# Local attention: queries scaled on GpSimd together with the keys, a constant scale in the mask, loops at fixed places

## The reference

```
q, k, v = split(shift_token(x) @ wqkv)          # 8 heads of 64
q = q / norm(q) * q_scale ;  k = k / norm(k) * k_scale
q, k = rotary_xpos(q, k)                        # q*cos*scale + rotate_half(q)*sin*scale, and the like
sim  = (8 * q) @ k.T   in windows of 64 keys and the 64 before, masked
x    = x + (softmax(sim) @ v) @ wo
```

## Time and profile before

| | |
|---|---|
| median of 3 runs | 1828.15 us (1822.93 to 1831.68) |
| the profiled execution | 1827.18 us, its span 1825.1 us |
| local attention, layer 0 | about 1085 to 1355 us of the span |
| local attention, layer 1 | about 1452 to 1740 us of the span |

### The profile page before, as it was taken

The page is one execution under the profiler, slowest core; times in us unless marked ns, Lnnn a source line. Parts: engine busy times, 40 slices in busy tenths (PEclk is TensorE's granted clock), DMA queues, the critical chain, the costliest instruction groups (busy, mean ns, idle before and its releaser), DMA issues. The chain is left out here.

```text
span 1825.1 us, 67884 instructions
## 1 busy us (share of the span) xinstructions
PE 1705.1 (93%) x27988; PEld 1021.4 (56%) x27988; DVE 1012.2 (55%) x3114; ACT 1415.4 (78%) x2635; POOL 453.6 (25%) x385
## 2 busy tenths in 40 slices
PE   7898899999998999999999978999989879999888
PEld 4674455555554555555555435666663346666633
DVE  5455533334342334333333058999975489999854
ACT  4343599999998999999999956888873369889842
POOL 1114000000000000000000027777830077877400
PEclk9898899999999999999999999999999989999999
DMA  2000311111111111111101030111110001111100
GB/s 60 3 1 26 107 49 51 62 44 63 63 49 45 55 44 63 63 56 57 49 31 44 3 110 18 33 36 32 23 36 11 0 18 32 25 34 32 33 15 35
DMA packets 47439, 73.56 MB, mean 40 GB/s; under 512 B 8401, under 2 KB 38225, under 8 KB 47185
## 3 DMA queue, kind: packets, MB, share of 16 engines
q1 hardware_dynamic: 47184, 69.85, 12.4%
HBM read 21.08 MB, written 2.10 MB: 13 GB/s over the span
## 5 line engine op out<-in xcount | busy, mean ns | idle before, releaser
L689 ACT ACTIVATE x_probs<-x_pss 128x1024 f32<-128x1024 f32 x832 | 806.3, 1021 | 54.8 <-PE x_pss L610 39.8
L624 PE MATMUL x_acc<-x_probs,x_v 128*32 128x256 f32 x6656 | 438.5, 381 | 0.0
L610 PE MATMUL x_pss<-x_qx,x_kx 32*128 32x256 bf16 x9984 | 350.8, 271 | 12.8 <-issue 5.7
L610 PEld LDWEIGHTS x_pss<-x_qx,x_kx 32*128 32x128 bf16 x9984 | 222.6, 93 | 200.0 <-ACT x_probs L689 180.5
L624 PEld LDWEIGHTS x_acc<-x_probs,x_v 128*32 128x32 f32 x6656 | 206.9, 110 | 93.4 <-issue 9.3
L736 DVE COPY x_vnext<-x_psp 128x128 f32<-128x128 f32 (+1 forms) x199 | 59.2, 297 | 316.5 <-PE x_psp L588 312.3
L1289 ACT ACTIVATE l_prob<-l_neg_sim,l_neg_top 128x128 f32<-128x128 f32 x512 | 198.2, 395 | 6.0 <-DVE l_neg_top L1180 6.0
L917 POOL TENSOR_TENSOR l_turned_half<-l_raw,l_tabB 128x512 f32<-128x512 f32 x128 | 185.8, 1473 | 50.4 <-ACT l_raw L1248 50.0
L665 POOL COPY x_zq<-zT 128x256 f32 (+1 forms) x15 | 6.0, 400 | 763.8 <-PE x_psp L595 693.6
L1180 DVE CUSTOM_DVE_ANT_0 l_neg_sim<-l_pss,w_window,l_inv_norm 128x128 f32<-128x128 f32 x512 | 148.8, 347 | 6.2 <-issue 5.5
L927 POOL TENSOR_TENSOR l_direct<-l_direct,l_turned_half 128x1024 f32<-128x1024 f32 x64 | 151.9, 2374 | 0.0
(11 more groups left out here) (184 smaller groups left out, 2593.6 us busy)
## 6 DMA issues: line engine op xcount, KB each, us to landing
x_kx<-x_kp SPq DMA_DIRECT2D x96, 208.0 KB, 2.3
x_cT<-in_context SPq DMA_DIRECT2D x16, 832.0 KB, 4.6
x_qx<-x_qp SPq DMA_DIRECT2D x48, 192.0 KB, 3.0
l_vmid<-l_vt SPq DMA_DIRECT2D x64, 128.0 KB, 2.3
xT<-in_x SPq DMA_DIRECT2D x8, 256.0 KB, 4.6
shifted<-zT SPq DMA_DIRECT2D x32, 64.0 KB, 2.0
hs<-zT SPq DMA_DIRECT2D x32, 64.0 KB, 2.0
out_x<-xT SPq DMA_DIRECT2D x8, 256.0 KB, 2.0
```

The costliest lines, as they stand in the source:

```text
L610: ins = pe.matmul(pss[bank(k, 2 * p + r // 2)][:, r % 2, e, :], kx[par][rows, g, j * P:(j + 1) * P], qx[par][rows, g, a * S:(a + 1) * S], ...
L624: ins = pe.matmul(acc[32 * r:32 * r + 32, 0:S], v[:, j, g, r, :], probs[SLOT[p]][r // 2][:, r % 2, e, :], start=(u == 0), stop=(u == UNITS ...
L689: act.activation(probs[SLOT[p]][y][:, :, :, :], pss[bank(k, 2 * p + y)][:, :, :, :], ACT.Sigmoid, scale=HD ** -0.5).then_inc(weighed, 1)
```

## The change

- scale_keys becomes scale_both: GpSimd multiplies all of direct (128x1024, queries and keys) by the inverse norms of both. It stands at the same place in GpSimd's order.
- flip_q waits for this scaling where it waited for join. flip_q(n+1, 0) is moved behind project_out(n-1), just ahead of flip_k(n+1, 0).
- mask takes the constant 1.0 as its scale where it had the pointer to inv_norm, and no longer waits for the inverse norms.
- The loops of GpSimd, VectorE and ScalarE in local_attention take two turns a pass (six passes) and no longer four (three passes); TensorE keeps four. These loops and those of norm_and_gate are loaded so that the loop's first instruction stands at slot 0 of a block of instructions.

```diff
--- before.py
+++ after.py
@@ -34,6 +34,11 @@
 HID = 341
 HC = (HID + P - 1) // P
 FAR = 3.0e38
+
+
+def aligned_loop(nc, eng, times):
+
+    return nc.Fori(0, times, engines=bass.OrderedEngineSet([eng.engine]), head_slot={eng.engine: 0})
 
 
 def shift_in(sp, shifted, zT, landed, n):
@@ -857,13 +862,13 @@
             n, r, q = x
             return n + by, (r + by) % 4, q + (r + by) // 4
 
-        def turns(eng, body):
+        def turns(eng, body, per):
 
             for n in range(-2, 2):
                 body((n, n % 4, n // 4))
-            with eng.Fori(0, 3) as i:
-                for k in range(2, 6):
-                    body((4 * i + k, k % 4, i + k // 4))
+            with aligned_loop(nc, eng, (B - 4) // per) as i:
+                for k in range(2, 2 + per):
+                    body((per * i + k, k % 4, i + k // 4))
             for n in range(B - 2, B + 1):
                 body((n, n % 4, n // 4))
 
@@ -927,28 +932,28 @@
                     pool.tensor_tensor(direct[r % 2][t][:, :, :], direct[r % 2][t][:, :, :], turned_half[t][:, :, :],
                                        ALU.add).then_inc(joined, 1)
 
-            def scale_keys(x, t):
+            def scale_both(x, t):
 
                 if exists(x):
                     n, r, _ = x
                     pool.wait_ge(newton, 4 * n + 4)
                     pool.wait_ge(joined, 2 * n + t + 1)
-                    pool.tensor_tensor(direct[r % 2][t][:, FH:QK, :], direct[r % 2][t][:, FH:QK, :],
-                                       inv_norm[r % 2][:, t, FH:QK].unsqueeze(2).broadcast_to([P, FH, FD]),
+                    pool.tensor_tensor(direct[r % 2][t][:, :, :], direct[r % 2][t][:, :, :],
+                                       inv_norm[r % 2][:, t, :].unsqueeze(2).broadcast_to([P, QK, FD]),
                                        ALU.mult).then_inc(scaled[t], 1)
 
             def turn(x):
                 turn_halves(later(x, 1), 1)
                 join(later(x, 1), 0)
                 turn_halves(later(x, 2), 0)
-                scale_keys(later(x, 1), 0)
+                scale_both(later(x, 1), 0)
                 join(later(x, 1), 1)
-                scale_keys(later(x, 1), 1)
+                scale_both(later(x, 1), 1)
 
             pool.memset(moved_to[64:P, :].rearrange("p (b s) -> p b s", s=S)[:, :, 0:1], 0.0).then_inc(first_cleared, 1)
             pool.wait_ge(first_cleared, 1)
             pool.wait_ge(ready, 2)
-            turns(pool, turn)
+            turns(pool, turn, 2)
 
         @block.tensor
         def _(pe):
@@ -993,7 +998,7 @@
             def flip_q(x, t):
                 if exists(x):
                     n, r, _ = x
-                    pe.wait_ge(joined, 2 * n + t + 1)
+                    pe.wait_ge(scaled[t], n + 1)
                     if t == 1:
                         pe.wait_ge(placed_q, 2 * n + 1)
                     elif exists(later(x, 1)):
@@ -1091,17 +1096,17 @@
                 turn_over(later(x, -1), 1, 1, x)
                 score(x, 1)
                 value(later(x, -1), 1)
-                flip_q(later(x, 1), 0)
                 turn_over(x, 0, 0)
                 project_k(later(x, 2), 1)
                 project_out(later(x, -1))
+                flip_q(later(x, 1), 0)
                 flip_k(later(x, 1), 0)
                 flip_q(later(x, 1), 1)
                 turn_over(x, 0, 1)
                 flip_k(later(x, 1), 1)
                 project_v(later(x, 1), 0)
 
-            turns(pe, turn)
+            turns(pe, turn, 4)
 
         @block.vector
         def _(dve):
@@ -1171,14 +1176,12 @@
                     n, r, _ = x
                     c = 4 * n + 2 * b + h
                     dve.wait_ge(scored, 2 * n + b + 1)
-                    if h == 0:
-                        dve.wait_ge(newton, 4 * n + 4)
                     at_least(dve, exped, c - 3)
                     at_least(dve, masked, c)
                     dve.memset(beat[:, :], 0.0)
                     for head in range(HALF * h, HALF * h + HALF):
                         ins = dve.tensor_tensor_reduce(out=neg_sim[b][:, head, :], in0=pss[head % 2][:, head // 2, :],
-                                                       in1=w["window"][:, b, :], scale=inv_norm[r % 2][:, b, head:head + 1],
+                                                       in1=w["window"][:, b, :], scale=1.0,
                                                        scalar=FAR, op0=ALU.add, op1=ALU.min,
                                                        accum_out=neg_top[b][:, head:head + 1])
                     ins.then_inc(masked, 1)
@@ -1229,7 +1232,7 @@
                                   w[scales][:, :, :].rearrange("p m d -> p (m d)").unsqueeze(1).broadcast_to([P, 2, 2 * FD]),
                                   ALU.mult).then_inc(ready, 1)
             dve.wait_ge(ready, 2)
-            turns(dve, turn)
+            turns(dve, turn, 2)
 
         @block.scalar
         def _(act):
@@ -1320,7 +1323,7 @@
                 place_queries(later(x, 1), 1)
 
             act.preload_act_table_set("natural_log_exp_and_others")
-            turns(act, turn)
+            turns(act, turn, 2)
 
 
 def norm_and_gate(nc, tag, norms, gates, zT, hs, w, moved, layer, xT=None, out=None, stored=None, next_shift=None):
@@ -1368,7 +1371,7 @@
         def chunks(eng, body):
 
             body(0, 0)
-            with eng.Fori(0, NCH // 2 - 1) as i:
+            with aligned_loop(nc, eng, NCH // 2 - 1) as i:
                 for u in range(2):
                     body(2 * i + 1 + u, 1 - u)
             body(NCH - 1, 1)
@@ -1524,7 +1527,7 @@
             guess(1)
             act.preload_act_table_set("gelu_and_others")
             act.wait_ge(bias_ready, layer + 1)
-            with act.Fori(0, NCH) as n:
+            with aligned_loop(nc, act, NCH) as n:
                 for c in range(HC):
                     act.wait_ge(up, passes + HC * n + c + 1)
                     act.activation(gelu[c][:, :], psg[c][:, :], ACT.Gelu,
```

## The result

The changed kernel takes 1879.66 us (median of 4 runs, 1878.15 to 1883.20), the kernel before 1827.61 in the same comparison (1822.93 to 1831.68). The ratio is 1.0288, 95% interval 1.0259 to 1.0318: slower, by 52 us where 43 were forecast, and inside the range.

What follows compares the result with a forecast made beforehand. VectorE, without gaps, was taken to set the 16.32 us batch; the change makes it 8.5 + 9.24 = 17.74, and 32 x 1.42 less about 2 us on 1827.2 gives 1870.6 us (1871 against the median), range 1840 to 1902.

Steps and rivals of the forecast that it cites:

- The chain from inv_norm to place_keys: Local attention: longer GpSimd scalings delay tile 1's flips, so place_keys comes at about 8.5 us after inv_norm, not 7.03.
- The collision of join with the norm: VectorE's norm and GpSimd's join exclude each other on SBUF, holding back tile 1's scaling by some 0.35 us (0 to 0.6).
- The moved flip_q of tile 0: On TensorE, behind project_out: its followers come some 1.2 us later, hidden under the wait or adding 0.1 us.
- The faster rival: Local attention: longer scalings stay hidden and cheaper masks shorten a batch to 15.42 or 15.6 us, about 1799 or 1804; chance 0.08.
- the no-change rival: Local attention: gain and wait cancel, with place_keys near 7.5 us after inv_norm, about 1828 us; chance 0.06.
- The mask's constant: VectorE's 16 masks a batch get 51 to 56 ns cheaper, 0.9 us; nearly all lost under the wait and at floor_of.
- the 9.24 us behind place_keys: VectorE's part of a batch from place_keys to the next inv_norm: 9.29 less 0.45 for masks plus 0.40 lost at floor_of.
- The sum: Both attention layers: 32 batches at +1.42 us, 45.4, less about 2 us of mask time in the last turns.
- The loops: Attention and gate loops: aligned loops gain 0; entering them costs 0 to 5 us in all, taken as 0.
- a sign of a cost left out: A longer gate stage or a pause at a loop's first pass would show a loop cost the forecast omitted.

Runs made afterwards that it cites:

- e1_mid: The changed kernel with flip_q of tile 0 one step earlier on TensorE, ahead of project_out: 1874.58 us, 1.0270 of the kernel before.
- e2_keys_only: The changed kernel with GpSimd scaling only the key half, the queries' norms left out: 1870.84 us, 1.0219 of the kernel before.
- e12_changed_pointer_mask: The changed kernel with the pointer to inv_norm back as the mask's scale, so queries are scaled twice: 1882.32 us, 1.0306 of the kernel before.
- e7_constant_mask_alone: The kernel before with only the mask's scale made constant 1.0, the queries' norms left out: 1826.32 us, 0.9997 of the kernel before.
- e9_before_one_input: e7_constant_mask_alone with VectorE's norm replaced by a reduction and floor_of by a memset: 1806.04 us, 0.9889 of the kernel before.
- e11_joins_first_mid_one_input: e4_joins_first_mid with VectorE's norm replaced by a reduction and floor_of by a memset: 1818.64 us, 0.9957 of the kernel before.
- e4_joins_first_mid: The changed kernel with both joins ahead of the scalings and flip_q of tile 0 ahead of project_out: 1858.30 us, 1.0173 of the kernel before.
- e6_old_loops: The changed kernel with the loops of the kernel before: 1884.49 us, 1.0323 of the kernel before.
- e5_new_loops_alone: The kernel before with only the changed kernel's loops: 1827.05 us against 1824.03, ratio 1.0019.
- e8_split: e4_joins_first_mid with each join and each scale_both cut into two 128x512 instructions: 1861.36 us, 1.0199 of the kernel before.
- e3_joins_first: The changed kernel with both GpSimd joins ahead of the scalings: 1929.60 us, 1.0556 of the kernel before.

## Why the prediction was right, and where its steps were off

**The chain from inv_norm to place_keys: right.** TensorE waits for GpSimd ahead of flip_q of tile 1, and every station came within 0.1 us. The scaling takes 1.90 us alone (1.89 forecast) and 2026 ns on average. The collision of join with the norm was to put back its end by 0.35 us; tile 1's scaling takes 2.17, so 0.27.

**The moved flip_q of tile 0: right for this kernel, not carried into the rivals.** The prediction let its followers hide under the wait or add 0.1, with a norm behind turn_halves that ends at about 8.6. It ended at 8.59, and e1_mid, where it ends earlier, gains 0 to 0.1 us a batch. But these followers are a second chain of nearly the same length: e2_keys_only has 17.48 us a batch with GpSimd as quick as before. The faster rival and the no-change rival asked only for a quicker chain to the flips, and that run shows that with the flip moved a quicker scaling alone would not have brought them about. That the two chains end together did not make the total: e1_mid has the loss without the second.

**The mask's constant: right.** 61 ns an instruction were saved (51 to 56 forecast). Half of it was to be lost under the wait and 0.40 of the other half in floor_of; that went from 0.18 to 0.63 us, and e12_changed_pointer_mask shows the constant to be worth 0.1 us a batch at most in the changed kernel.

**The faster rival: mis-sized.** It gave 15.4 to 15.6 us a batch if the scalings stayed hidden. e7_constant_mask_alone is that case and has 16.30, and without collisions e9_before_one_input still has 16.03. VectorE without a gap did not mean that VectorE's own work set the pace: the lengthened instructions among it took up what was saved. The 16.03 and 16.05 of the runs without collisions come with short waits of VectorE, 0.44 us for ScalarE's raw in e9_before_one_input and 0.47 for a flip in e11_joins_first_mid_one_input. TensorE is then the fullest engine, busy for 61.79 of 64.12 us over four batches of the former, and waits 0.34 us a batch for placed keys; which cycle holds them was not tested and stays open.

**The no-change rival: its point was wrong.** place_keys at 7.5 gives 17.25 us a batch, not 16.3. The prediction took the 9.24 us behind place_keys as fixed; in e4_joins_first_mid they are 9.77, as a norm in that part met GpSimd.

**The sum: 7.1 us short in attention, and 5.8 outside it.** The steady batches fit: twelve distances in each layer grew by 17.7 and 17.5 us, where 12 x 1.42 is 17.0. The ends did not: from the stage's start to the first add +6.4 and +3.5, over the last three batches +2.5 each, so 8.9 and 6.0 where the sum had 4 x 1.42 less 1, or 4.7.

The loops are not the cause of that, for e6_old_loops has 58.83 and 57.55 us from the stage's start to the first add, the changed kernel 58.99 and 57.65, and before 52.61 and 54.12. e4_joins_first_mid has 54.17 and 53.07, so most of it goes with the order of the work. The granted clock over this part fell from 0.90 to 0.82 in layer 0 and from 0.87 to 0.85 in layer 1, which the sum did not have; how much of the 6.4 us that is was not taken apart. The loops' pauses come later, inside the twelve distances. The sum had the loops at 0, and e5_new_loops_alone measures 3.0 us for them, 0.5 to 6.2 by its interval, against a bound of 5.

Outside attention there are +2.8 us ahead of it and +3.0 in the last gate. Nothing ahead of attention was changed, and over the fourteen kernels its start lies anywhere between 1077.0 and 1089.0 us. In the last gate VectorE does stand still at a loop, which the prediction had named as a sign of a cost left out:

```profile
1821.70 0.75 DVE L1489 SCALAR_TENSOR_TENSOR g_gated<-g_mean,g_bias,g_gelu 128x512 f32<-128x512 f32 x1 [2.46 <-issue]
```

Yet this is not shown to be the 3.0 us: the last gate took 84.66 us before, 87.64 after, and 87.44 in e7_constant_mask_alone, which has the loops of before. The profiled execution was also one of the longer ones (1883.20 against the median 1879.66). The median is 8.7 us over the forecast.

## What to carry to other kernels

Lay out the cycle, that is, which instruction waits for which from one batch to the next, before giving work to an engine that looks idle: GpSimd was idle for a fifth of a batch, but its last scaling ended 0.17 us before the flips would have waited for it. Follow a moved instruction through every engine to the end of its followers before calling it covered, and don't take the rest of the cycle as fixed, for instructions that exclude each other meet at new places. The price of a saving comes from a run in which that saving is made alone.

## What the runs showed of the hardware

- An instruction of 0.18 us (floor_of, 128x32, two inputs) took 0.63 us where it came during turn_halves, and 922 ns on average in e8_split. The norm, 0.69 us alone, lost 0.82 us (1.51) during turn_halves in the same batch. A short instruction can lose about as much as a long one.
- Cutting GpSimd's 128x1024 instructions in two did not shorten VectorE's waits as a whole (a batch 17.25 us uncut, 17.43 cut).
- Two passes of a loop lost 5.3 and 5.8 us in one kernel (e6_old_loops), and none did in another with the same loops (before); near a loop's entry an engine stood still for up to 2.96 us.
- TensorE stood idle for 2.87 us in each batch of e3_joins_first, and its granted clock fell from 1.00 to 0.50 soon after it took up work again. The stretch from the scores to the next turn_over took 5.42 us, and 3.77 in the changed kernel at a clock of 1.00.
